# Prologue and last step of a two-layer conditional MoE kernel rearranged: first-layer weights of batch 0 mixed on two engines, batch 0 unrolled, last `down` in PSUM banks of its own

## The reference

```python
# layer 0: 8 weight matrices mixed by y = cond_8[b], times a mask
masked_w = weight * mask[None, :, :]
w_bot = jnp.einsum('bg,got->bot', y, masked_w)
x = x + jnp.einsum('bnt,bot->bno', x, w_bot) + bias
# layer 1: softmax of cond_8, the best two experts, and a shared MLP
def _gemma_mlp(x, gate_w, up_w, down_w):
    g = jnp.einsum('bsh,hi->bsi', x, gate_w)
    u = jnp.einsum('bsh,hi->bsi', x, up_w)
    return jnp.einsum('bsi,ih->bsh', jax.nn.gelu(g, approximate=True) * u, down_w)
x = x + sum_e w[b, e] * _gemma_mlp(x, expert e) + _gemma_mlp(x, shared)
```

## Time and profile before

| | kernel before |
|---|---|
| median of 3 runs | 432.74 us |
| lowest, highest | 432.04, 435.02 us |
| span of the profiled execution | 431.0 us |
| TensorE busy | 416.2 us, 97% |
| VectorE busy | 263.8 us, 61% |
| ScalarE busy | 180.6 us, 42% |
| GpSimd busy | 137.1 us, 32% |
| mean granted clock of TensorE | 0.992 |

### The profile page before, as it was taken

How to read it: one execution, slowest core, us unless ns; L and a number is a source line. 1 busy time by engine, 2 the same in 40 slices (tenths; PEclk the granted TensorE clock), 3 DMA queues, 4 the chain that set the end, 5 groups by cost and what they waited for, 6 DMA issues and landing times.

```text
span 431.0 us, 5433 instructions
## 1 busy us (share of the span) xinstructions
PE 416.2 (97%) x1810; PEld 342.1 (79%) x1810; DVE 263.8 (61%) x340; ACT 180.6 (42%) x288; POOL 137.1 (32%) x78
## 2 busy tenths in 40 slices
PE   8649999999999999999999999999999999999996
PEld 7338888888888888888888888888888888888885
DVE  5797687657535686765634787765733556656543
ACT  2512645544322544535432454543532254454521
POOL 0681445334100245443300135433500034434400
PEclk9988999999999999999999999999999999999999
DMA  7854223322202123321301132332210122310001
GB/s 266 333 173 132 73 82 103 108 76 74 75 0 97 37 86 96 110 80 66 110 0 41 56 97 86 110 86 70 100 37 0 50 73 77 108 37 1 2 0 49
DMA packets 14780, 35.04 MB, mean 81 GB/s; under 512 B 1840, under 2 KB 2864, under 8 KB 14768
## 3 DMA queue, kind: packets, MB, share of 16 engines
q1 hardware_dynamic: 14768, 34.89, 25.5%
HBM read 32.79 MB, written 2.10 MB: 81 GB/s over the span
## 4 chain that ended last, share of the span: by engine, by line
PE 92%; DVE 4%; DMA 1%; issue 1%; ACT 0%; SPq 0%; DVEq 0%; ACTq 0%
PE o_ps L289 30%; PE u_ps L271 20%; PE g_ps L271 20%; PE u_ps L277 10%; PE g_ps L277 10%; PE l_ps L241 2%; DVE sh_hi L523 1%; DMA l_raw<-l_w 1%; PE l_ps L246 1%; DVE l_acc L424 1%; DVE x_lo L450 0%; DVE pair_sum L398 0%; DVE probs L396 0%; DVE l_lo L437 0%; ACT x_hi L330 0%
## 5 line engine op out<-in xcount | busy, mean ns | idle before, releaser
L536 POOL TENSOR_TENSOR ex_lo<-raw,ex_hi 128x768 fp32r<-128x768 f32 x64 | 117.9, 1842 | 257.8 <-ACT ex_hi L346 257.8
L468 DVE TENSOR_TENSOR h_lo<-h,h_hi 128x512 fp32r<-128x512 f32 x96 | 131.9, 1374 | 66.0 <-ACT h_hi L349 66.0
L340 ACT ACTIVATE gelu<-g_ps 128x512 f32<-128x512 f32 x96 | 57.4, 598 | 165.4 <-PE g_ps L277 165.2
L465 DVE SCALAR_TENSOR_TENSOR h<-gelu,route_cur,u_ps 128x512 f32<-128x512 f32 x64 | 47.8, 747 | 62.3 <-ACT gelu L340 62.1
L349 ACT CAST h_hi<-h 128x512 fp32r<-128x512 f32 x96 | 59.7, 622 | 50.4 <-DVE h L460 30.5
L346 ACT CAST ex_hi<-raw 128x768 fp32r<-128x768 f32 x64 | 52.9, 827 | 0.0
L271 PE MATMUL g_ps<-x_hi,ex_hi 128*128 (+1 forms) x128 | 49.8, 389 | 0.0
L271 PE MATMUL g_ps<-x_hi,ex_lo 128*128 (+1 forms) x128 | 49.8, 389 | 0.0
L271 PE MATMUL u_ps<-x_hi,ex_hi 128*128 (+1 forms) x128 | 49.8, 389 | 0.0
L271 PE MATMUL u_ps<-x_hi,ex_lo 128*128 (+1 forms) x128 | 49.8, 389 | 0.0
L289 PE MATMUL o_ps<-h_hi,ex_hi 128*128 128x512 f32 x128 | 49.8, 389 | 0.0
(11 more groups left out here) (67 smaller groups left out, 547.5 us busy)
## 6 DMA issues: line engine op xcount, KB each, us to landing
raw<-experts SPq DMA_DIRECT2D x64, 384.0 KB, 3.0
raw<-shared SPq DMA_DIRECT2D x8, 384.0 KB, 9.1
l_raw<-l_w SPq DMA_DIRECT2D x4, 512.0 KB, 5.6
x_in<-xT SPq DMA_DIRECT2D x8, 256.0 KB, 3.3
outT<-out_sb SPq DMA_DIRECT2D x4, 256.0 KB, 2.0
outT<-out_sb SPq DMA_DIRECT2D x8, 128.0 KB, 1.9
mask<-l_mask SPq DMA_DIRECT2D x1, 256.0 KB, 7.0
cond_all<-cond SPq DMA_DIRECT2D x1, 16.0 KB, 3.4
```

The source lines that it names most:

```text
L340: act.activation(gelu[:, s % 2], g_ps[:, s % 2], ACT.Gelu_apprx_tanh).then_inc(gelu_done, 1)
L465: dve.scalar_tensor_tensor(h[:, s % 2], gelu[:, s % 2], route_cur[:, k:k + 1], u_ps[:, s % 2], ALU.mult, ALU.mult).then_inc(h_done, 1)
L468: dve.tensor_tensor(h_lo[:, s % H_SLOTS], h[:, s % 2], h_hi[:, s % H_SLOTS].bitcast(F32), ALU.subtract).then_inc(h_lo_done, 1)
L536: pool.tensor_tensor(lo, raw[:, slot], hi.bitcast(F32), ALU.subtract).then_inc(w_lo_done, 1)
```

## The change

All of it lies in the prologue, in batch 0 and in the last step.

- **Loads.** Slabs of `l0_w` one by one, the halves of x between them, the mask in two halves; `cond` and bias on ScalarE's queue.
- **Mixing for batch 0.** VectorE mixes only the half oh = 0 (`combine_0`, one instruction per matrix, scalars straight from `cond_all`). For oh = 1, GpSimd makes an identity matrix, ScalarE scales it by each of the eight weights (`scale_ident`, into `diag`, which is `out_sb`'s memory), and TensorE sums the eight products in PSUM (`mix_l0`, plain fp32 matmuls of 256 columns). The mask is applied to that PSUM tile.
- **x added by TensorE.** `pass_x`: four matmuls of an fp32r identity with `x_hi`, `x_lo` open the sums in `l0_ps`; `first_layer_0` adds its 12. `x1_hi` is made by ScalarE from PSUM with the bias, `x1_lo` by VectorE from PSUM, and x1 itself later by ScalarE (`first_x1`).
- **Warm-up.** 12 matmuls of zeros instead of 34, then single 256-column ones between the mixes, then 6 of 256 and 4 of 512 columns.
- **Chunks 0 and 1** are split in three parts each. All hi copies of shared chunks are ScalarE's, chunks 3 to 7 one in each of steps 0 to 4.
- **Routing.** The index search stands just ahead of `step(0, 0)`; the eight operations of the weights stand by twos behind steps 2 to 5 of batch 0.
- **Batch 0** is written out ahead of the loop on ScalarE and VectorE (loop of batches 1 and 2); on TensorE, GpSimd and SP the loops are as before.
- **Last step.** Its `down` writes `LAST_PS`, banks of `l0_ps` and `g_ps`, in three pieces; VectorE first adds x1 and `o_ps` (after the `down` before it), then each piece.

```diff
-WARM_UP = 34
+WARM_UP = 12
@@ SP
+            for g in range(2):
+                load_l0(g)
+            load_x_half(0, 0)
+            for g in range(2, 4):
+                load_l0(g)
+            load_x_half(0, 1)
+            for g in range(4, G):
+                load_l0(g)
@@ TensorE
+            def mix_l0(g):
+                pe.wait_ge(diag_done, g + 1)
+                pe.wait_ge(l0_in[g], 16)
+                mm = pe.matmul(mix_ps, diag[:, g], l0_raw[:, g, D:2 * D], start=(g == 0), stop=(g == G - 1))
...
+            keep_warm(WARM_UP, P, T)
+            for g in range(G):
+                mix_l0(g)
+                if g < G - 1:
+                    keep_warm(1, P, T // 2)
+            keep_warm(6, P, T // 2)
+            keep_warm(4, 3 * P // 4, T)
+            pass_x()
+            first_layer_0()
@@ TensorE, last step
+            def last_down():
+                s = STEPS - 1
+                w_hi, w_lo = weights(s)
+                pe.wait_ge(h_lo_done, STEPS * B)
+                for ps, (oh, tokens) in zip(LAST_PS, OUT_PIECES):
...
+                    mm.then_inc(last_down_done, 1)
@@ ScalarE, prologue
+            for g in range(2):
+                scale_ident(g)
+            act.wait_ge(routed, ROUTED_SHIFTED)
+            act.activation(exps[:], shifted[:], ACT.Exp).then_inc(exp_done, 1)
+            for g in range(2, G):
+                scale_ident(g)
...
+            for hh in range(HH):
+                split_x(0, hh)
+            for oh in range(HH):
+                split_l0(0, oh)
+            split_part(0, GATE)
+            split_part(0, UP)
+            act.wait_ge(bias_in, 16)
+            first_x1_hi(0)
+            split_part(1, GATE)
+            first_x1_hi(1)
+            split_part(1, UP)
+            split_part(0, DOWN)
+            split_part(1, DOWN)
+            for oh in range(HH):
+                first_x1(oh)
+            split_shared(FIRST)
@@ ScalarE, in step, between gelu and h_hi
+                if isinstance(b, int) and b == 0 and FIRST + 1 + s < CHUNKS:
+                    split_shared(FIRST + 1 + s)
@@ VectorE, prologue
+            route_top()
+            for g in range(4):
+                combine_0(g)
+            split_x(0, 0)
+            for g in range(4, G - 1):
+                combine_0(g)
+            split_x(0, 1)
+            combine_0(G - 1)
...
-            route_weigh()
-            for c in range(ACT_SHARED, CHUNKS):
-                dve.wait_ge(raw_in[c], 16)
-                dve.tensor_copy(sh_hi[:, c], raw[:, c]).then_inc(sh_hi_done, 1)
...
+            route_index()
             step(0, 0)
@@ VectorE, end
+            def store_last():
+                dve.wait_ge(stored, 16 * len(OUT_PIECES) * (B - 1) + 1)
+                dve.wait_ge(down_done, STEPS * B - 1)
+                at = ((B - 1) % 2) * (HH * T)
+                for hh in range(HH):
+                    dve.tensor_tensor(out_sb[:, hh], x1[:, at + hh * T:at + (hh + 1) * T], o_ps[:, hh], ALU.add).then_inc(rest_done, 1)
+                for i, (ps, (hh, tokens)) in enumerate(zip(LAST_PS, OUT_PIECES)):
+                    dve.wait_ge(rest_done, hh + 1)
+                    dve.wait_ge(last_down_done, i + 1)
+                    dve.tensor_tensor(out_sb[:, hh, tokens], out_sb[:, hh, tokens], ps, ALU.add).then_inc(last_out_done, 1)
```

More of the change, by code:

```diff
@@ L131, in build @@
         l0_ps = psum("l0_ps", [P, HH, T])
+        LAST_PS = [l0_ps[:, 0], l0_ps[:, 1, 0:T // 2], g_ps[:, 0, 0:T // 2]]
+        mix_ps = u_ps[:, 1, 0:D]
+        idle_ps = g_ps[:, 1]
         zeroed = sem("zeroed")
+        ident_done = sem("ident_done")
+        ident_r_done = sem("ident_r_done")
+        diag_done = sem("diag_done")
+        mixed = sem("mixed")
         cond_in = sem("cond_in")
[L135 to L136 removed]
+        l0_in = [sem(f"l0_in{g}") for g in range(G)]
+        mask_in = [sem(f"mask_in{oh}") for oh in range(HH)]
         bias_in = sem("bias_in")
@@ L209, in _ @@
             sp.sem_inc(stored, 1)
[L210 to L215, removed]
+            for g in range(2):
[7 more added lines that the diff above has]
+            for oh in range(HH):
+                sp.dma_start(mask[:, oh * D:(oh + 1) * D], l0_mask[oh]).then_inc(mask_in[oh], 16)
             for c in range(CHUNKS):
                 sp.dma_start(raw[:, c % RAW_SLOTS], shared[c]).then_inc(raw_in[c % RAW_SLOTS], 16)
-            sp.wait_ge(routed, ROUTED_IDX)
+            sp.wait_ge(indexed, B)
             e = expert_of(0, 0)
@@ L292, in down @@
                 mm.then_inc(down_done, 1)
+            def last_down():
[3 more added lines that the diff above has]
+                for ps, (oh, tokens) in zip(LAST_PS, OUT_PIECES):
+                    at = DOWN + oh * P
+                    for i, (w, x) in enumerate(((w_hi, h_hi), (w_hi, h_lo), (w_lo, h_hi))):
+                        mm = pe.matmul(ps, w[:, at:at + P], x[:, s % H_SLOTS, tokens], start=(i == 0), stop=(i == 2))
+                    mm.then_inc(last_down_done, 1)
             def batch(b, with_next):
@@ L367, in _ @@
                 split_x(0, hh)
-                split_l0(0, hh)
-            for c in range(ACT_SHARED):
-                split_weights(c, sh_hi[:, c])
-                if c < HH:
-                    split_x1(0, c)
-            with act.Fori(0, B - 1) as b:
+            for oh in range(HH):
+                split_l0(0, oh)
[8 more added lines that the diff above has]
+            split_part(1, DOWN)
+            for oh in range(HH):
+                first_x1(oh)
+            split_shared(FIRST)
+            batch(0, True)
+            with act.Fori(1, B - 1) as b:
                 batch(b, True)
@@ new lines, in apply_mask_0, with first_x1_lo @@
+            def apply_mask_0(oh):
+                dve.wait_ge(mask_in[oh], 16)
+                if oh == 0:
+                    dve.wait_ge(combined, G)
+                    mix = half(l0_acc, 0)
+                else:
+                    dve.wait_ge(mixed, 1)
+                    mix = mix_ps
+                dve.tensor_tensor(half(l0_acc, oh), mix, half(mask, oh), ALU.mult).then_inc(masked, 1)
+            def first_x1_lo(oh):
+                dve.wait_ge(x1_hi_done, oh + 1)
+                dve.scalar_tensor_tensor(x1_at(x1_lo, 0, oh), l0_ps[:, oh], bias[:, oh:oh + 1], x1_at(x1_hi, 0, oh).bitcast(F32), ALU.add, ALU.subtract).then_inc(x1_lo_done, 1)
```

217 lines of the change are left out of this document (144 added, 73 removed).

## The result

The changed kernel is faster, by less than half of what was forecast. Its median is 428.35 us (428.10 to 428.47, 4 runs) against 432.39 us (432.01 to 435.02, 4 runs) of the kernel before beside it: ratio 0.9891, interval 0.9864 to 0.9918. The forecast was 422.7, range 421.0 to 426.5. In a later group of runs the same kernel had 428.11, ratio 0.9876 (0.9851 to 0.9900). The profiled span fell from 431.0 to 426.0 us, and it is the account of these 5.0 us that the following is about.

The account below looks back on a forecast made before the run. TensorE was taken to bound the kernel, busy 97% of the span, leaving head and tail to move: 431.0 - 10.7 + 0.65 = 421.0 us profiled; with the median 1.7 above the span, 422.7 us, range 421.0 to 426.5.

Parts of the forecast that it names:

- what bounds the kernel: TensorE, busy 97% of the span, at 4.08 us a step; only the head and the tail can move.
- the main gain: Casts and routing weights leave VectorE's way and the head shortens: `gate_up(0,3)` at 26.3 instead of 36.98, 10.7 us gained.
- Nothing: Parts forecast to cost or gain no time: separate semaphores, masks in halves, unrolling, and the index at SP's later wait.
- (c): Batch 0: VectorE becomes the bound, blocked by GpSimd's splits; 4.7 us lost, 427.4 us; chance 0.06.
- Its own sign of being wrong: Batch 0: the forecast counts as wrong if u_ps waits for h there; no wait over 0.5 us was expected.
- Head: Prologue up to the first `gate_up`: `gate_up(0,0)` starts at 16.6 instead of 17.86.
- it should land at about 10.5: Prologue loads: last slab of `l0_w` lands at about 10.5, with 2,560 KB in the queue including itself.
- From there: From `gate_up(0,0)` at 16.6: `gate_up(0,2)` at 22.2 after 0.15 us of waiting, `gate_up(0,3)` at 26.3.
- Tail: Last step: VectorE's two added additions delay the final three adds; 0.65 us longer, bounds 0 and 0.9.
- (a): Warm-up and mixing: TensorE's clock falls, 6.9 us at half rate cost 3.4, giving 426.1 us; chance 0.10.
- (b): Prologue mixing: fp32 matmuls take 1.2 us each, the eight end at 16.2 instead of 11.05; 427.8 us; chance 0.08.
- (d): Prologue mixing: the eight fp32 matmuls don't overlap, 2.3 us each; +14 us, 436.7 us, slower than before; chance 0.04.

Follow-up runs that it names:

- The two kernels that mend the failed steps: Changed kernel with x and routing weights early, no ten fillers, old tail: 423.16 us, ratio 0.9763; that with `cond` and bias on SP: 422.50 us, ratio 0.9748.

## Why the prediction was wrong

**Right: what bounds the kernel, and the main gain.** `gate_up(0,3)` was to come 10.7 us earlier and came 8.9 earlier. The wait of 5.89 us for `h(0)` is gone, and so is the low clock of the earlier trace rows. Nearly all of it is the casts and the routing weights: with these and x early it comes 36.98 - 28.62 = 8.4 earlier.

**Wrong: "the index moved to SP's later wait is covered, since experts' slots come free only with sh_lo".** This sentence, listed under *Nothing*, is the step that failed. It is true of the index, and it names the very thing that costs: expert slots come free only with `sh_lo`. It stops at the index instead of asking what else SP has behind those slots. The change moved the cast of chunk 7 to step 4, thus `sh_lo(7)` to 38.52, thus the last slot's load, and the load of x for batch 1 stood behind it on SP's queue: 41.20 where before it was issued at 35.12. The rule of following a moved step through every queue was applied to VectorE and ScalarE, not to SP. Price: 2.7 us, shown by the kernel with x early (1.3 once VectorE's delay is gone too).

**Wrong: no stall in batch 0 from VectorE.** Rival (c) had the mechanism (GpSimd blocks VectorE) and took it as a sum over six steps, 4.7 us. Moving the routing weights away gives 2.1 us, 0.7 once x is early: combines and routing operations do get blocked for about 1.6 us each, but only two or three times where h is late. The forecast took them at nothing, where (c)'s rows had shown 1.75 for `pair_sum`. Its own sign of being wrong, that u_ps waits for h in batch 0, came true at 41.29 and 52.25.

**Head, forecast 16.6, measured 17.96.** By its terms:

- The last mix starts at 12.17 instead of 10.5. The size of a mix was right: with the 256-column filler between, one starts every 0.68 us against 0.55 + 0.11:

```profile
10.11 0.67 PE L230 MATMUL u_ps<-l_raw,out_sb 128*128 128x256 f32 x2 [0.55 <-DMA l_raw<-l_w]
...
10.80 0.67 PE L230 MATMUL u_ps<-l_raw,out_sb 128*128 128x256 f32 x2
...
11.48 0.67 PE L230 MATMUL u_ps<-l_raw,out_sb 128*128 128x256 f32 x2
12.17 0.67 PE L230 MATMUL u_ps<-l_raw,out_sb 128*128 128x256 f32 x2
```

  What was wrong is the slabs' arrival: "SP's first issue is no longer `cond`, so it should land at about 10.5". The last slab landed at 12.04. The spacing was right, 0.67 to 0.71 us from one transfer to the next, but the row of them began late: reckoned back from 10.5 by nine times 0.67 the first slab should have landed at 4.5, and it landed at 5.89. The sixteen parts of a slab had drifted apart: those of the fifth came in from 8.59 to 9.97, where in the kernel before the fourth pair's came from 9.09 to 9.57. The spread is there in `cond` on the other queue (3.10 to 5.25) and in the first slab (4.34 to 5.89), and with `cond` first on SP's queue the first slab's is 4.56 to 4.88. So the move that was to save an issue made `cond` 1 us later and the slabs with it. Putting it back, together with the bias, gave 0.44 us at `gate_up(0,0)`. Part of why it doesn't give the whole 1.4 is the late transfer behind the fourth slab, whose cause is open.
- From the last mix's start to `pass_x` 14.31 - 12.17 = 2.14, forecast 0.55 + 1.9 = 2.45. Without the ten fillers `pass_x` starts 1.8 us sooner, so their size was right, but they were not needed (0.87 us at `gate_up(0,0)`).
- `pass_x` and the first layer took 17.96 - 14.31 = 3.65, forecast 3.6.

**From there** to `gate_up(0,3)`: 28.10 - 17.96 = 10.1, forecast 9.7; 0.3 of it lies ahead of `gate_up(0,2)`.

**Tail, forecast +0.65, measured +0.5.** The mechanism is as told: VectorE's two added additions stand before the three that matter.

```profile
420.50 0.40 PE L332 MATMUL l_ps<-h_hi,ex_hi 128*128 128x512 f32 x1
...
420.76 1.28 DVE L597 TENSOR_TENSOR out_sb<-x,o_ps 128x512 f32<-128x512 f32 x2 [0.49 <-PE o_ps L320]
421.19 0.28 PE L332 MATMUL l_ps<-h_hi,ex_hi 128*128 128x256 f32 x1
...
421.31 0.28 PE L332 MATMUL l_ps<-h_lo,ex_hi 128*128 128x256 f32 x1
...
421.97 1.01 DVE L601 TENSOR_TENSOR out_sb<-out_sb,l_ps 128x512 f32<-128x512 f32 x2
...
422.68 1.32 SPq L200 DMA_DIRECT2D outT<-out_sb  x3
```

The first addition waits for the `down` before, 0.49 us, and the three adds can't begin before 421.97, with SP's first issue 2.18 us after the last `down` begins against 427.62 - 425.96 = 1.66 before. The six 256-wide matmuls start 0.12 us apart, not 0.19: the weight load of 0.188 does not bound them.

**The sum.** -10.7 was -8.9, the tail +0.65 was +0.5, and +3.4 in batch 0 was missing: 431.0 - 8.9 + 3.4 + 0.5 = 426.0. Of the 5.0 us by which the span was missed 3.4 are batch 0, 1.4 the head and 0.4 the way to `gate_up(0,3)`, less 0.2 in the tail. The median lies 2.35 us above the profiled span, not 1.7. The two kernels that mend the failed steps land where the forecast lay, at 423.2 and 422.5.

**The rivals.** (a), the clock, did not come in the changed kernel. (b) and (d), a dear fp32 matmul, are refuted by the 0.68 us between mixes, filler included. The forecast's low price held: a mix shows as two rows, and the 0.68 us fit its 0.55 with 0.11 for the filler. The range missed because none of its cases was a late transfer, and the cases that would have reached beyond it, (b) at 427.8 and (c) at 427.4, were given 0.14 together and left outside.

## What to carry to other kernels

When work that frees a buffer is moved later, look up which load waits for that buffer, and then every load behind it on the same queue, of whatever data: here the load that hurt shared nothing with the moved cast but the queue. A change with many parts is to be tried in parts: the casts and routing weights alone beat the whole, and of the rest two parts were losses (fillers 0.9 us, tail 0.5). An operation of 8 elements is not free next to GpSimd, but the blocking cost time here only where the result was already late.

## What the runs showed of the hardware that was not expected

- The same 16 KB load of `cond` was used at 5.27 us when issued from ScalarE's queue at 0.79, beside SP's slabs, and at 4.32 when issued first on SP's queue at 0.86; the second slab was used 1.05 us earlier too. A transfer's sixteen parts do not come in together: beside `cond` on the other queue those of the first slab spread over 4.34 to 5.89, behind `cond` on the same queue over 4.56 to 4.88, and in all nine profiles of kernels with `cond` on ScalarE's queue those of the fifth slab spread over 1.4 to 1.9 us, against 0.5 for a pair in the kernel before. Why `cond` delays some parts and not others was not settled.
- A 1 KB load (bias) on the second queue came with a dip: 142 to 158 GB/s from 4 to 5 us in eight profiles, 344 in the one with the bias moved. Removing it brought the fifth slab no earlier, since its last part came no earlier.
- An fp32 matmul of 128x128 by 256 columns shows as two rows. With a filler of 256 columns behind it one starts every 0.68 us, and in places every 0.55 (8.21 and 8.76 in the kernel with `cond` and bias on SP); an fp32r one of 256 columns with new weights each time starts every 0.12 us.
- TensorE's granted clock fell to 0.50 (1.2 GHz) at about 15.2 us in one profile in which TensorE had waited 1.97 us and then 0.81 us, and stayed at 1.00 with waits of 1.53 and 0.81, and of 1.21 and 0.81.
